# Three context products a scan step instead of four, and half of the context values made in two later stages

## What is computed

```python
def step(state, bc):                      # 512 steps, one after another
    b_t, c_t = bc
    s = state @ A_bar + b_t
    s = _layernorm(s, ln_st_g, ln_st_b)
    return (s, c_t * s)
...
ssm = ssm @ D_w.T + D_b
return ssm * gate
...
xn = layer_norm(x, g1, b1)                # x is the context here
ln = layer_norm(latents, g2, b2)          # the latents are the tokens
q = ln @ Wq
kv = jnp.concatenate([xn, ln], axis=1) @ Wkv
```

## Time and profile before

| | us |
|---|---|
| median of 2 runs | 5576.16 |
| lowest and highest | 5573.18, 5579.15 |
| the profiled execution, its own time | 5576.56 |
| its span, first to last instruction | 5573.9 |

### The profile page before, as it was taken

The page is one execution under the profiler, slowest core; times in us unless marked ns, Lnnn a source line. Parts: engine busy times, 40 slices in busy tenths (PEclk is TensorE's granted clock), DMA queues, the critical chain, the costliest instruction groups (busy, mean ns, idle before and its releaser), DMA issues. The chain is left out here.

```text
span 5573.9 us, 78192 instructions
## 1 busy us (share of the span) xinstructions
PE 5019.0 (90%) x23756; PEld 2573.1 (46%) x23756; DVE 3869.1 (69%) x7722; ACT 2858.9 (51%) x6162; POOL 2482.0 (45%) x1470
## 2 busy tenths in 40 slices
PE   5699998589999979789958999999999999999955
PEld 3455555323333346433324555555555555555523
DVE  6666665788888747788865666666666666666588
ACT  3466666147677733357643444444444444444423
POOL 3455555300000011100025777777777777787800
PEclk9899999779999979989978999999999999999978
DMA  3477776232232100733224333333333333333200
GB/s 128 146 250 244 243 250 219 98 105 70 61 74 63 48 0 0 243 90 76 68 92 115 95 84 85 85 91 95 91 84 87 88 91 95 88 86 84 56 32 21
DMA packets 392210, 574.44 MB, mean 103 GB/s; under 512 B 35968, under 2 KB 251328, under 8 KB 390912
## 3 DMA queue, kind: packets, MB, share of 16 engines
q1 hardware_dynamic: 389248, 566.60, 36.2%
q10 hardware_dynamic: 2688, 4.46, 0.2%
HBM read 316.93 MB, written 220.20 MB: 96 GB/s over the span
## 5 line engine op out<-in xcount | busy, mean ns | idle before, releaser
L2312 POOL TENSOR_TENSOR la_acc<-la_acc,la_pr 128x1024 f32<-128x1024 f32 x704 | 1696.4, 2410 | 497.7 <-ACT la_pr L2270 462.4
L2270 ACT ACTIVATE la_pr<-la_s_ps 128x512 f32<-128x512 f32 x1536 | 793.7, 603 | 972.5 <-PE la_s_ps L2122 970.8
L2129 PE MATMUL la_o_ps<-la_pr,la_vf 128*64 128x512 f32 x3072 | 743.8, 605 | 0.0
L1519 DVE TENSOR_REDUCE ca_mx<-ca_m_ps 128x1 f32<-128x512 f32 x1024 | 638.7, 682 | 95.1 <-PE ca_m_ps L1337 90.9
L2121 PE MATMUL la_s_ps<-la_q_hl,la_k_hh 128*128 128x512 f32 x1536 | 691.8, 450 | 1.6 <-ACT la_q_hs L2246 1.4
L1490 ACT ACTIVATE ca_pr<-ca_s_ps 128x512 f32<-128x512 f32 x1024 | 540.9, 600 | 221.2 <-PE ca_s_ps L1352 216.3
L2339 DVE TENSOR_REDUCE la_mx<-la_m_ps 128x2 f32<-128x1024 f32 x384 | 462.6, 1205 | 216.9 <-PE la_m_ps L2104 208.5
L2122 PE MATMUL la_s_ps<-la_q_hs,la_k_l 65*128 65x512 f32 x1536 | 609.0, 396 | 0.0
L2339 DVE TENSOR_REDUCE la_mx<-la_misc 128x2 f32<-128x1024 f32 x384 | 465.9, 1213 | 0.0
L107 POOL TENSOR_TENSOR ff_ln_var_eps<-ff_ln_mv,g_eps 128x4 f32<-128x4 f32 x32 | 6.7, 208 | 1012.1 <-DVE ff_ln_mv L92 1012.1
L1337 PE MATMUL ca_m_ps<-ca_ks,ca_qs 96*128 96x512 bf16 x1024 | 403.5, 395 | 5.0 <-DVE ca_mx L1519 4.9
(11 more groups left out here) (368 smaller groups left out, 8609.3 us busy)
## 6 DMA issues: line engine op xcount, KB each, us to landing
la_k_hh<-scratch_k_high SPq DMA_DIRECT2D x128, 512.0 KB, 6.5
scratch_xv<-sc_v_full SPq DMA_DIRECT2D x128, 256.0 KB, 2.7
scratch_k_high<-sc_k_high SPq DMA_DIRECT2D x128, 256.0 KB, 2.6
scratch_k_low<-sc_k_low SPq DMA_DIRECT2D x128, 256.0 KB, 3.0
la_w_parts<-scratch_w_parts SPq DMA_DIRECT2D x64, 512.0 KB, 6.3
la_k_l<-scratch_k_low SPq DMA_DIRECT2D x64, 512.0 KB, 8.4
la_vf<-scratch_xv SPq DMA_DIRECT2D x64, 512.0 KB, 4.1
ca_ks<-scratch_kstack SPq DMA_DIRECT2D x64, 384.0 KB, 6.2
```

Source lines behind the costliest of these rows:

```text
L1519: dve.tensor_reduce(mx[:, u % 2, qt, h, half:half + 1], m_ps[:, turn_of(u, i, NM)[0], :], AX.X, ALU.max).then_inc(m_reduced, 1)
L2129: last = pe.matmul(o_ps[XD * h:XD * h + XD, :], vf[:, par, st, XD * h:XD * h + XD], pr[:, st % LAG, h, :], start=(st == 0), stop=(st == XT ...
L2270: act.activation(pr[:, st % LAG, h, :], s_ps[:, (2 * st + h) % 3, :], ACT.Exp, scale=scale).then_inc(p_done, 1)
L2312: pool.tensor_tensor(total, total, exps, ALU.add).then_inc(acc_done, 1)
```

## The change

- `scan`: `PER_STEP` goes from 4 to 3, a round has 16 jobs (four of the first layer, then values and keys in the pattern `vkkvkkvkkvkk`), so every one of the 32 steps has three products. A value job now makes the first 512 value columns of 128 rows only. ACT keeps a job every second step. SP's order is rewritten: the last two key stores of a round come in the next one, both stores of the scan's own states stand at new places, and the next round's `n_parts` are loaded after the round's last step. POOL splits the next context ahead of the keys.
- A class `ContextValues` makes the other 512 value columns: per 512 context rows two loads of 512 KB, 24 products, four keeps on ACT and four stores of 256 KB. `ssm_outputs` does this for rounds 0 to 7 and `latent_inputs` for rounds 8 to 15, one in each batch.
- `ssm_outputs` also stores the split value weights (`xv_parts`) and the split key weights that `scan` has on chip, and splits and stores the query weights. `latent_inputs` no longer splits weights; it loads `xv_parts`.
- Loops of both phases are unrolled.

```diff
-JOBS, JOB_SLOTS, JOB_BANKS, PER_STEP = 4 + 2 * XPAIRS, 6, 6, 4
+JOB_ORDER = "abcdvkkvkkvkkvkk"
+JOBS, JOB_SLOTS, JOB_BANKS, PER_STEP = len(JOB_ORDER), 6, 6, 3
...
+                    if n:
+                        store_k(n - 1, 6)
+                        store_k(n - 1, 7)
                     store_values(n)
+                    store_keys(n)
                     store_v(n, 0)
-                    store_keys(n)
+                    keep(n, 0)
...
+                    keep(n, 1)
                     if n + 1 < rounds:
                         sp.wait_ge(job_ready, JOBS * (n + 1))
                         load_normed(n + 1)
...
+class ContextValues:
+    def load(self, sp, i):
+        n = self.chunks[i]
+        if i >= 2:
+            sp.wait_ge(self.ready, NT * (i - 1))
+        for part, src in enumerate((self.io["norm_t"], self.io["ctx_low"])):
+            sp.dma_start(...).then_inc(self.loaded[i % 2], 16)
+    def project(self, pe, i, xv):
+        pe.wait_ge(self.loaded[i % 2], 32 * (i // 2 + 1))
+        for t in range(NT):
+            if i:
+                pe.wait_ge(self.kept, NT * (i - 1) + t + 1)
+            for y, (k, w_part, n_part) in enumerate(products):
+                last = pe.matmul(self.banks[:, t, :], ...)
+            last.then_inc(self.ready, 1)
+    def keep(self, act, i):
+        for t in range(NT):
+            act.wait_ge(self.ready, NT * i + t + 1)
+            if i:
+                act.wait_ge(self.stored[t], 16 * i)
+            act.activation(self.kept_v[:, t, :], self.banks[:, t, :], ACT.Copy).then_inc(self.kept, 1)
+    def store(self, sp, i):
+        for t in range(NT):
+            sp.wait_ge(self.kept, NT * i + t + 1)
+            sp.dma_start(...)
...
 ssm_outputs, SP:
                 def batch(b, par, it, has_next):
                     if has_next:
-                        sp.wait_ge(y_step, Y_STEPS * b)
+                        if b:
+                            sp.wait_ge(y_step, Y_STEPS * b)
                         load(b + 1, 1 - par)
+                    if b == 0:
+                        values.load(sp, 1)
+                        sp.dma_start(io["xv_parts"], w.xv[:, :, :, :].bitcast(F32)).then_inc(parts_stored, 16)
+                        for part in range(2):
+                            for k in range(KD):
+                                store_parts_of(1, part, k, w.xk[:, part, k, :])
+                    values.store(sp, b)
+                    if b + 2 < B:
+                        values.load(sp, b + 2)
...
+                sp.wait_ge(q_high_done, 1)
+                sp.wait_ge(q_low_done, KD)
+                for k in range(KD):
+                    store_parts_of(0, 0, k, q_high[:, k, :])
+                    store_parts_of(0, 1, k, q_low[:, k, :])
...
 ssm_outputs, PE, at the end of a batch:
                     last.then_inc(o_ready, 1)
+                    values.project(pe, b, w.xv)
 ssm_outputs, ACT, behind y_t of batch b:
+                    if b:
+                        values.keep(act, b - 1)
 ssm_outputs, POOL, behind the add to x of batches 1 and 2:
+                        pool.tensor_tensor(q_low[:, b - 1, :], q_raw[:, b - 1, :], ...)
...
 latent_inputs, ACT, behind the store of the turned tokens of batch b:
+                    if b:
+                        values.keep(act, b - 1)
 latent_inputs, POOL, at the end:
-                for i in range(2):
-                    pool.wait_ge(w_high_done, i + 1)
-                    pool.tensor_tensor(w_low[:, i, :, :], w_qk[:, i, :, :], ...)
```

More of the change, by code:

```diff
@@ L755, in _ @@
                         load_normed(n + 1)
-                    store_v(n, 7)
-                    store_k(n, 7)
-                    keep(n, 1)
+                for p in (6, 7):
+                    store_k(rounds - 1, p)
                 sp.wait_ge(k_stored, 16 * STORES * rounds)
@@ L926, in _, with __init__, wait @@
                         dve.reciprocal(r[:, :], sigma[:, :]).then_inc(r_ready, 1)
+class ContextValues:
+    def __init__(self, nc, ctx, semctx, tag, io, chunks):
+        pool = Pools(nc, ctx, tag + "_cv")
+        self.io, self.chunks = io, chunks
+        self.parts = pool.sb("parts", [P, 2, 2, KD, T], F32R)
+        self.kept_v = pool.sb("kept_v", [P, NT, T])
+        self.banks = pool.ps("banks", [P, NT, T])
+        self.ready, self.kept = sems(nc, semctx, tag + "_cv", "ready kept")
+        self.loaded = sems(nc, semctx, tag + "_cv", "loaded_even loaded_odd")
+        self.stored = sems(nc, semctx, tag + "_cv", " ".join(f"stored_{t}" for t in range(NT)))
+    def load(self, sp, i):
[3 more added lines that the diff above has]
+        for part, src in enumerate((self.io["norm_t"], self.io["ctx_low"])):
+            sp.dma_start(self.parts[:, i % 2, part, :, :].bitcast(F32),
+                         src[n // 2][:, :, n % 2 * T:(n % 2 + 1) * T]).then_inc(self.loaded[i % 2], 16)
+    def project(self, pe, i, xv):
+        products = [(k, w_part, n_part) for w_part, n_part in ((0, 0), (1, 0), (0, 1)) for k in range(KD)]
+        pe.wait_ge(self.loaded[i % 2], 32 * (i // 2 + 1))
[3 more added lines that the diff above has]
+            for y, (k, w_part, n_part) in enumerate(products):
+                last = pe.matmul(self.banks[:, t, :], self.parts[:, i % 2, n_part, k, t * P:(t + 1) * P], xv[:, w_part, k, T:2 * T],
+                                 start=(y == 0), stop=(y == len(products) - 1))
+            last.then_inc(self.ready, 1)
[6 more added lines that the diff above has]
+    def store(self, sp, i):
+        n = self.chunks[i]
+        for t in range(NT):
+            sp.wait_ge(self.kept, NT * i + t + 1)
+            sp.dma_start(self.io["xv"][n // 2, XPAIRS // 2:XPAIRS, :, n % 2 * NT + t, :].rearrange("u p n -> p u n"),
+                         self.kept_v[:, t, :].rearrange("p (u n) -> p u n", u=XPAIRS // 2)).then_inc(self.stored[t], 16)
+    def wait(self, sp):
+        for t in range(NT):
+            sp.wait_ge(self.stored[t], 16 * len(self.chunks))
@@ L970, in _ @@
                 pe.wait_ge(w_loaded, 32)
-                with pe.Fori(0, B) as b:
+                for b in range(B):
                     pe.wait_ge(y_step, Y_STEPS * (b + 1))
@@ L981, in _ @@
                     last.then_inc(o_ready, 1)
+                    values.project(pe, b, w.xv)
             @block.scalar
             def _(act):
-                with act.Fori(0, B) as b:
+                for b in range(B):
                     act.wait_ge(yT_ready, b + 1)
@@ L1053, in _ @@
                 normed_state(1, 1, 0)
-                batches(dve, batch)
+                batches_unrolled(batch)
 def attention_inputs(nc, io, g, semctx, tag, own_keys, wq, wk, wv, bq, bk, qstack, kstack, vaug):
```

142 lines of the change are left out of this document (79 added, 63 removed).

## The result

The kernel before took 5576.2 us, the changed one 5635.1 us: a ratio of 1.0106, 95% interval 1.0062 to 1.0149. The prediction was 5617.

| stretch | before | after | difference | predicted |
|---|---|---|---|---|
| `scan` | 706.1 | 629.5 | -76.6 | -83.3 |
| from its end to the first memset of `ssm_outputs` | 4.3 | 6.9 | +2.6 | +2.7 |
| `ssm_outputs`, to the start of the next stage | 75.8 | 163.5 | +87.7 | +88 |
| inputs of the first attention | 91.7 | 92.2 | +0.5 | 0 |
| first attention (tiles `ca_`), from its first to its last max product | 800.8 | 822.3 | **+21.5** | **0** |

The account below looks back on a forecast made before the run. PE's products were taken to set the step of `scan`, the stage to be relieved. Terms: 5576.6 - 83.3 + 2.7 + 88 + 33 = 5617.0 us; 5555 to 5665 should hold 8 of 10.

Parts of the forecast that it names:

- `scan`, -83.3: `scan`: three products a step instead of four bring it from 706.1 to 622.8 us.
- The step of 1.20: `scan`: the recurrence ends last instead of PE's products, so a step takes 1.20 us instead of 1.34.
- the keep that just fits: `scan`: ACT's keep of 0.57 us, one in two steps, ends at 611.13, before line 919 ends at 611.14.
- rival 3: `scan`: `n_parts` comes two us late at each round's start, +30 us, 5647 in all; chance 0.10.
- rival 2: `scan`: PE's gaps bring the lower clock throughout, steps of 1.81 us, 312 us more, 5929; chance 0.05.
- The end, +2.7: End of `scan`: the last key job's keep, split, store and landing stand alone, +2.7 us, between 0 and +6.
- `ssm_outputs`, +88: `ssm_outputs`: `u` queued on SP behind value stores makes a batch 18.6 us against 8.2; +88 us in all, ends +50 and +110.
- The tail: End of `ssm_outputs`: last products, keep, store and query weight stores take 25 us against 10 before, +15.
- `latent_inputs`, +33: `latent_inputs`: batches of 11.5 us against 6.5, +35 for seven intervals, 2 less at the end; ends +18 and +70.
- The wait of 2.6: `latent_inputs`: PE stands still 2.6 us a batch until ACT's first keep of the batch before.
- Everything else, 0: Stages that the change doesn't touch, the first attention among them: predicted difference 0.
- Rival 1: `ssm_outputs`, `latent_inputs`: moved products mostly hide, `u` landing 2.3 us after issue; costs about 56 and 22, 5574 us; chance 0.30.

Follow-up runs that it names:

- e3: Changed kernel with SP issuing the load of `u` for batch b+2 ahead of batch b's value stores in `ssm_outputs`; 5573.8 us, ratio 1.0002.
- c2: c1 plus key and value weight halves stored in `scan`, query weights split ahead of the first batch and stored from batch 3; 5520.9 us, ratio 0.9900.
- e1: Changed kernel with DVE's list of `ssm_outputs` a loop over two batches again, other engines unchanged; 5614.8 us, ratio 1.0076.
- e2: Kernel before with DVE's list of `ssm_outputs` written out batch by batch, same instructions in the same order; 5590.6 us, ratio 1.0035.
- c4: c2 with 60 instructions that only wait added on ACT behind `y_t` in the batches of `ssm_outputs`; 5516.5 us, ratio 0.9894.
- c1: Changed kernel with DVE's loop restored, `u` loaded ahead of the stores, and ACT's keeps first in both stages; 5539.5 us, ratio 0.9935.

## Why the prediction was right, and where it fell short

The forecast's direction, its reasons and two of its four terms held. That the four add up to +40.4 forecast and +40.2 measured is luck: `scan` won 6.7 us less than said, and `latent_inputs` cost 6.5 less.
- **`scan`, -83.3, measured -76.6.** The step of 1.20, the keep that just fits, no late `n_parts` (rival 3) and the clock (rival 2) came as said. The term was mis-sized: 510 steps at 1.20 left out the 1.37 at the end of each 16, 5.0 us. A row of the end of such a list, read before, would have shown it.
- **The end, +2.7, measured +2.6.**
- **`ssm_outputs`, +88, measured +87.7**, and by the mechanism named, which e3 proves by taking it away. Within it errors cancel. Five batches cost 58 and not 54 with `q_low`, which counted in full for two of them (2.1 each), where I took half. The tail cost 11.7 and not 15, the first two batches 17.7 and not 19. A product at the higher clock, 0.27 in the forecast, took 0.25 (24 in 6.00).
- **`latent_inputs`, +33, measured +26.5.** The mechanism held, the sizes didn't. The wait of 2.6 was 2.9 and a batch took 10.5, not 11.5. I set all seven intervals against 6.5, where the last was 14.7 already, so they cost 19.8 and not 35; and I gave the end 2 us less, where it cost 6.9 more, since the split of 8.99 had stood ahead of the last transposes and not behind them. These two errors, 15.2 too dear and 8.9 too cheap, cancel for the larger part. I had the products of a batch at 6.5, all at the higher clock, and left the lower one to the range: five bursts of eight started low, for 6 to 14 of their 24 products, and a burst took 5.7 to 8.6 us at 0.80 granted in the stretch.
- **Everything else, 0, measured +18.** This is the step that failed: I cut the kernel into the stages that the diff touches and took all others as fixed. They were, to the operation, but not their places in the instruction lists. By the packets (some 10 a turn after the change, 5 in c2, none before), DVE's loop (306 instructions) and ACT's (292) were each fetched again in every turn. Up to the last max product DVE's part is 16 to 18 us (e1, e2) and ACT's 5.4 (c4 against c2); with what comes back in the rest of the attention they are 14 and 3. Of that return the traces show the size and that it comes and goes with the stalls (56.1 us again in c4), not the reason.
- **Rival 1 (0.30).** Its mechanism, `u` overtaking the queue, is not there: 5.3 us from issue to landing, 2.3 in the earlier trace rows. But its result, that the moved products mostly hide, is what the same kernel gives once the order on SP is right.

## What to carry to other kernels

Work moved into a stage with idle engines is paid by what its transfers and copies are queued ahead of, not by the engines' shares: follow each in-order queue (SP, ACT) through one batch, and put the load that the next batch waits for ahead of stores that nobody waits for (`ssm_outputs` took 163.5 us with `u` behind the stores and 104.3 with it ahead, and 127.2 with ACT's keeps first). When a stage that was not edited gets slower, look at the packets of kind "instruction" and at idle time that ends in "issue" at a loop's first instruction; an edit anywhere ahead on the same engine's list may have moved a long loop (32 places on DVE cost 17 us here, 60 on ACT 5.4). And before thinning out a matmul stream, ask whether what is left still keeps the clock (three products a step kept 0.99, one had 0.62 and cost 43 us).

## What the runs showed that I had not expected

- A loop of 306 instructions on DVE, 292 on ACT, was fetched again in each turn or not at all, by its place, as far as packets of kind "instruction" tell: on DVE shifts of 0, 16 and 96 instructions gave 7 instruction packets in the stretch, 32 and 64 gave 37 or 38, some 5 packets a turn. On DVE that is a stall of 2.9 us a turn, and the attention pays all of it up to its last max product (17.6 us of stalls, 818.1 against 800.5, in e2); on ACT a turn is 0.9 us longer. Length alone doesn't do it: PE's turn has 1136 rows in the trace, 568 weight loads and 568 matmuls, and before the change the attention moved 15 instruction packets in all, 7 of 8 KB and 8 of 16 KB.
- DVE stands beside a large instruction of POOL: in `ssm_outputs` its four `so_y` take 0.87 us alone, 2.9 beside one POOL instruction of 2.34 and 5.0 beside two; in `latent_inputs` before, 9.65 instead of 1.35 beside 8.99.
- 120 instructions on PE that only wait, on a semaphore already reached, took 0.11 us each, and put off the first transposes by 8.6 us.
- Four stores of 512 KB behind one of 2 MB kept SP busy for 15.0 us of issue alone in the changed kernel (line 1022). There its first value store was ready only as they ended; in the quicker c1 the same stores held up the next two batches.
